# A graph layer and a mixture of experts in one kernel: spreading one group's layer-norm work over four expert tiles

## What is computed

```
x = x + gnn(layernorm(x), adj)                  # first half of the program
u = layernorm(x)
topk_vals, topk_idx = top_k(u @ gate_w + gate_b, 2)
topk_w = softmax(topk_vals)
h = relu(u @ w1[e] + b1[e]);  expert_out = h @ w2[e] + b2[e]
y = u + sum over the two chosen experts of topk_w * expert_out
x = x + layernorm(y) * gamma + beta             # the second layer norm is the group work of this study
```

## Time and profile before

| | us |
|---|---|
| median of 3 runs | 888.42 |
| lowest and highest run | 888.24, 890.37 |
| the profiled execution | 883.51 |
| span of its trace | 881.0 |

### The profile page before, as it was taken

One profiled execution on the slowest core, in us unless ns is written; L12 is line 12 of the kernel. 1 busy time (PEld: TensorE's weight loads), 2 busy tenths in 40 slices (PEclk: granted clock), 3 DMA queues, 4 the chain that ended last, 5 costly groups with the idle time before them and its releaser, 6 DMA issues. The chain is left out here.

```text
span 881.0 us, 20052 instructions
## 1 busy us (share of the span) xinstructions
PE 771.3 (88%) x4739; PEld 590.4 (67%) x4740; DVE 619.3 (70%) x2448; ACT 527.7 (60%) x1123; POOL 550.9 (63%) x572
## 2 busy tenths in 40 slices
PE   5999999999999999961899999988878888888844
PEld 4577777777777777751677777766656666666621
DVE  3688999999999998866455554567665666665648
ACT  2599999999999999871233333444443343343435
POOL 2005777777677777675777777777765565565630
PEclk9999999999999999995899999999998889898969
DMA  5323343333333332215777667888887778767636
GB/s 153 97 73 109 120 122 121 118 121 116 105 118 116 119 95 75 74 58 146 215 207 199 199 206 238 260 239 231 247 239 215 225 215 236 216 198 221 188 131 215
DMA packets 104175, 145.23 MB, mean 165 GB/s; under 512 B 17537, under 2 KB 56855, under 8 KB 104119
## 3 DMA queue, kind: packets, MB, share of 16 engines
q1 hardware_dynamic: 84582, 109.16, 44.0%
q0 software_dynamic: 17344, 34.13, 11.1%
q10 hardware_dynamic: 2192, 1.31, 0.5%
HBM read 99.67 MB, written 46.81 MB: 166 GB/s over the span
## 5 line engine op out<-in xcount | busy, mean ns | idle before, releaser
L471 POOL DMA_INDIRECT combined<-tout,tdest x286 | 285.7, 999 | 129.9 <-issue 74.0
L458 POOL DMA_INDIRECT dispatched<-rows,slot_i x256 | 259.5, 1014 | 165.5 <-issue 145.6
L795 ACT ACTIVATE hid<-bank,wts 128x256 f32<-128x256 f32 x286 | 119.6, 469 | 236.5 <-PE bank L651 235.8
L1119 DVE SCALAR_TENSOR_TENSOR tout<-bank,gate,tin 128x128 f32<-128x128 f32 x286 | 86.9, 345 | 157.9 <-PE bank L666 156.7
L666 PE MATMUL bank<-wts,hid 128*128 128x128 f32 x1144 | 175.5, 299 | 0.0
L666 PEld LDWEIGHTS bank<-wts,hid 128*128 128x128 f32 x1144 | 147.2, 201 | 17.8 <-issue 1.5
L651 PE MATMUL bank<-tut,wts 128*128 128x256 f32 x572 | 155.4, 396 | 0.0
L506 PEld LDWEIGHTS bank<-w_sb,work 128*128 128x128 f32 x1024 | 123.1, 194 | 17.9 <-issue 14.6
L506 PE MATMUL bank<-w_sb,work 128*128 128x128 f32 x1024 | 126.3, 277 | 2.1 <-ACT work L774 2.1
L500 PE MATMUL bank<-agg,w_sb 128*128 128x512 f32 x256 | 124.8, 610 | 0.0
L651 PEld LDWEIGHTS bank<-tut,wts 128*128 128x128 f32 x572 | 103.0, 201 | 8.7
(11 more groups left out here) (159 smaller groups left out, 1046.8 us busy)
## 6 DMA issues: line engine op xcount, KB each, us to landing
wts<-in_w_exp SPq DMA_DIRECT2D x143, 257.0 KB
tin<-dispatched SPq DMA_DIRECT2D x143, 132.0 KB
moe<-combined SPq DMA_DIRECT2D x32, 512.0 KB, 4.6
xs<-in_x SPq DMA_DIRECT2D x32, 256.0 KB, 3.2
adj_sb<-in_adj_t SPq DMA_DIRECT2D x32, 256.0 KB, 3.3
rms_b<-r_row SPq DMA_DIRECT2D x32, 256.0 KB, 3.2
out<-agg SPq DMA_DIRECT2D x32, 256.0 KB, 4.2
combined<-tout,tdest POOLq DMA_INDIRECT x286
```

The lines of the kernel that those rows point to most:

```text
L458: nc.gpsimd.indirect_dma_start(dispatched, bass.IndirectOffsetOnAxis(slot_i[:, k, n:n + 1], 0), rows[:, k, n // TOPK, n % TOPK, :], None). ...
L471: nc.gpsimd.indirect_dma_start(combined, bass.IndirectOffsetOnAxis(tdest[:, k, a:a + 1], 0), tout[:, k, a, :], None, bounds_check=TOK * TO ...
L795: last = nc.scalar.activation(hid[:, n % 2, c, :], hid_ps[n % 2][:, c * TILE:(c + 1) * TILE], ACT.Relu, bias=wts[:, k, F + FC * D + c:F + ...
L1119: last = nc.vector.scalar_tensor_tensor(out=tout[:, k, a, :], in0=exp_ps[n % 2][:, a * D:(a + 1) * D], scalar=gate[:, n % 2, a:a + 1], in1 ...
```

## The change

`post_step` gets an argument `quarters`. In `mixed` it is now called behind each of the four tiles, each time with one number from 0 to 3. VectorE has in quarter 0 the scale, the offset and the sum of the two halves, in quarter 1 the statistics, in quarter 2 the multiplication by gamma, in quarter 3 the last addition. ScalarE has two of its four activations in quarter 1, the other two and the square root in quarter 2. SP keeps its whole post step, in quarter 3. TensorE has nothing in these steps. The second part: `tut_ps` is now banks 0 and 1 in turn, so a transpose waits for the copy of two tiles back, not of the last one. `y_ps`, used in the tail, moves to banks 0 to 2.

```
-        tut_ps, hid_ps, exp_ps = bank[0], bank[2:4], bank[4:6]
-        y_ps = (bank[1], bank[6], bank[7])
+        tut_ps, hid_ps, exp_ps = bank[0:2], bank[2:4], bank[4:6]
+        y_ps = bank[0:RING]
...
                 for k in range(RING * GB):
                     tile_step(i, t + k, 2)
-                    if k % GB == GB - 1:
-                        post_step(i, g + k // GB)
+                    post_step(i, g + k // GB, (k % GB,))
...
# SP
-                if has(i, g):
+                if 3 in quarters and has(i, g):
...
# TensorE, tile_step
-                    if n >= 1:
-                        pe.wait_ge(t_ut, count(i, n, 1, RING2 * m))
+                    if n >= 2:
+                        pe.wait_ge(t_ut, count(i, n - 1, 1, RING2 * m))
                     for a in range(TH):
-                        last = nc.tensor.transpose(tut_ps[:, a * P:(a + 1) * P], tin[:, k, a, 0:D],
+                        last = nc.tensor.transpose(tut_ps[n % 2][:, a * P:(a + 1) * P], tin[:, k, a, 0:D],
                                                    ident[:])
...
# ScalarE, post_step
+                for half in range(2):
+                    if 1 + half in quarters and has(i, g):
...
+                        for j in (2 * half, 2 * half + 1):
+                            last = nc.scalar.activation(n3[:, k, j, :], y_of(i, g, k)[:, j, :], ACT.Identity,
+                                                        bias=nb[:, 0, k, j:j + 1], scale=rs[:, 0, k, j:j + 1])
+                        if half == 1:
+                            last.then_inc(p_n, 1)
...
-                if has(i, g):
+                if 2 in quarters and has(i, g):
                     k = g % RING
                     act.wait_ge(p_bn, count(i, g + 1))
...
# VectorE, post_step
                 g = t
-                if has(i, g):
+                if 0 in quarters and (i is not None or 0 <= g < MIXED):
+                    k = g % RING
+                    dve.wait_ge(moe_in[k], count(i, g // RING + 1, 16, 1))
+                    nc.vector.tensor_tensor(moe[:, k, :, 0, :], moe[:, k, :, 0, :], moe[:, k, :, 1, :],
+                                            ALU.add).then_inc(p_sum, 1)
+                if 1 in quarters and has(i, g):
```

More of the change, by code:

```diff
@@ L386, in _, with post_step @@
                 sp.wait_ge(scattered[k], 16 * GB * TOPK * len(range(k, NG, RING)))
-            def post_step(i, t):
+            def post_step(i, t, quarters=range(GB)):
                 g = t + 2
-                if has(i, g):
+                if 3 in quarters and has(i, g):
                     k = g % RING
@@ L798, in tile_step, with post_step @@
                     last.then_inc(t_relu, 1)
-            def post_step(i, t):
+            def post_step(i, t, quarters=range(GB)):
                 g = t - 1
-                if has(i, g):
[L803 to L811, removed]
+                for half in range(2):
+                    if 1 + half in quarters and has(i, g):
+                        k = g % RING
+                        if half == 0:
+                            if g >= RING:
+                                act.wait_ge(p_g, count(i, g - RING + 1))
+                            act.wait_ge(p_nb, count(i, g + 1))
+                            act.nop(nofuse=True)
+                        for j in (2 * half, 2 * half + 1):
[3 more added lines that the diff above has]
+                            last.then_inc(p_n, 1)
                 g = t
-                if has(i, g):
+                if 2 in quarters and has(i, g):
                     k = g % RING
@@ L816, in post_step @@
                     nc.scalar.activation(sd[:, 0, k, :], bn[:, 0, k, :, 2], ACT.Sqrt, bias=ln_eps[:, 0:1],
[L817 to L818 removed]
+                                         scale=1.0 / D).then_inc(p_sd, 1)
             tiles_and_groups(act, tile_step, post_step, -1)
@@ L1100, in tile_step @@
                         dve.wait_ge(t_h, count(i, n - 1, 1, RING2 * m))
-                    nc.vector.tensor_copy(tut[:, n % 2, :], tut_ps[:, 0:TILE]).then_inc(t_ut, 1)
+                    nc.vector.tensor_copy(tut[:, n % 2, :], tut_ps[n % 2][:, 0:TILE]).then_inc(t_ut, 1)
                 n = t - 1
@@ L1122, in tile_step, with post_step @@
                     last.then_inc(t_out, 1)
-            def post_step(i, t):
+            def post_step(i, t, quarters=range(GB)):
                 g = t - 1
-                if has(i, g):
+                if 0 in quarters and has(i, g):
                     k = g % RING
@@ L1129, in post_step @@
                     nc.vector.reciprocal(rs[:, 0, k], sd[:, 0, k, :]).then_inc(p_rs, 1)
-                g = t - 1
-                if has(i, g):
-                    k = g % RING
                     dve.wait_ge(p_rs, count(i, g + 1))
@@ L1137, in post_step @@
                 g = t
-                if has(i, g):
+                if 0 in quarters and (i is not None or 0 <= g < MIXED):
+                    k = g % RING
+                    dve.wait_ge(moe_in[k], count(i, g // RING + 1, 16, 1))
+                    nc.vector.tensor_tensor(moe[:, k, :, 0, :], moe[:, k, :, 0, :], moe[:, k, :, 1, :],
+                                            ALU.add).then_inc(p_sum, 1)
+                if 1 in quarters and has(i, g):
                     k = g % RING
                     if summed_by_dve(i, g):
-                        dve.wait_ge(moe_in[k], count(i, g // RING + 1, 16, 1))
-                        nc.vector.tensor_tensor(moe[:, k, :, 0, :], moe[:, k, :, 0, :], moe[:, k, :, 1, :],
-                                                ALU.add).then_inc(p_sum, 1)
                         dve.wait_ge(p_sum, count(i, g + 1))
@@ L1157, in post_step @@
                         .then_inc(p_g, 1)
-                g = t - 2
-                if has(i, g):
+                if 3 in quarters and has(i, g):
                     k = g % RING
```

## The result

| | before | after |
|---|---|---|
| median | 889.19 us (4 runs, 888.24 to 890.37) | 849.62 us (4 runs, 847.04 to 855.23) |
| profiled execution, span | 883.51, 881.0 | 847.04, 845.3 |

The changed kernel takes 0.956 of the time of the one before (95% interval 0.951 to 0.962), some 40 us less. The forecast was 851 us and a span of 844.

A forecast was written before the change was run, and what follows sets the result against it. VectorE's post-step lump stalls TensorE; beneath lie two floors, POOL's scatters and SP's loads. Their chains put the last scatter at 808.2 and 809.3, so 37 us off 888.4 gives 851 us; range for 8 in 10, 842 to 872.

The forecast's parts named there:

- The lump on VectorE and TensorE's wait for the copy: Mixed stretch: quarters of at most 1.1 us replace VectorE's 3.36 us lump; TensorE's 39.2 us wait should be nearly gone.
- the second edit's step: Two transpose banks: alone they only move the 2.01 us wait to the first product (L651); no term of its own.
- SP's wait for ScalarE: SP's load of moe waits for ScalarE's normalising; these 33.0 us should go nearly whole, below 5 us left.
- The load of `moe`, five tiles ahead instead of eight: The sum moves three tiles earlier, leaving the load at least 12.9 us against 4.6 us needed; costed at nothing.
- The two rivals without a gain: TensorE held at each quarter, 888 us, chance 0.05; VectorE waits for moe in quarter 0, slower, chance 0.05.
- POOL as one floor: Expert stretch: 285 scatter steps of 1.29 us plus contention put the last scatter's start at 808.2.
- 8.8 us of contention: POOL scatters starting inside VectorE additions of two SBUF operands: 0.4 us for each of 22 post steps.
- SP as the other floor: SP's load chain: without 33.0 us of waits and 3.6 us before the transpose, last scatter at 809.3.
- The tail moves as a whole: What follows the last scatter has unchanged code and moves 37 us earlier; span 844.
- What would make it wrong: Mean clock below 0.9, tiles waiting for tin over some 10 us in total, or VectorE waiting for moe.
- the other signs: POOL's tout waits below 20 us, 37 or 38 scatters per 50 us, last near 809, more long scatters, clock near 1.00.
- The third limit: Rival: DMA capped at 0.85 (866 us) or clock dropping once per group (873 us); together chance 0.25, 860 to 880.

The follow-up runs named there:

- half the scatters: Changed kernel with the second of each tile's two scatters left out and moe loaded from input x; 845.12 us, ratio 0.956 to the kernel before.
- paired reads: SP reads two tiles' table entries at once: changed kernel 853.98 us, ratio 0.968; also with half the scatters left out, moe from x, 842.45 us, ratio 0.954.
- ScalarE's transfers with operands in PSUM: Changed kernel with ScalarE issuing the post step's moe load and out store, and gamma, beta and their product in PSUM; 1125.44 us, ratio 0.982 to the kernel before.

## Why the prediction held, point by point

*The lump on VectorE and TensorE's wait for the copy* (3.36 us, 39.2 us in all): right. The quarters alone take the wait away; the banks alone only move it to L651, as the second edit's step said, and win what the transposes' head start is worth. Their bound was 0.4 us for each of 22 post steps, 9 us, and 10.5 us were measured, with an interval of 5 to 14.

*SP's wait for ScalarE*, 33.0 us: gone whole. SP's last load of rows was to be issued at 794.9 and was at 794.21.

*The load of `moe`, five tiles ahead instead of eight*, costed at nothing: right, no wait for `moe` shows. *The two rivals without a gain*, a copy late by a quarter and a VectorE that waits for `moe`, did not come.

*POOL as one floor*: right. It was to be busy from the first scatter to the last, and was. The step of 1.29 us plus 8.8 us of contention gave 376.5 us; it took 378.5. The excess over 0.98 us per scatter sums to 292.5 - 286 x 0.98 = 12.2 us. In 560 to 808 us, 34 scatters began inside one of the three instructions of a post step with two SBUF inputs, with over 0.1 us of it left, and took 1.21 us in the mean, which makes 34 x 0.23 = 7.8 us; the others took 0.997 us, which makes 2.5 us more. That rest has the same cause, in an instruction that the argument had left out, the addition of beta to `xs`, 128x128 and with two SBUF inputs too:

```profile
710.27 1.20 POOL L470 DMA_INDIRECT combined<-tout,tdest  x1 [0.31 <-issue]
710.30 0.28 DVE L1111 TENSOR_TENSOR xs<-xs,beta_sb 128x128 f32 x1
```

All scatters of the expert stretch that took over 1.00 us began inside one of these four instructions or at most 0.03 us ahead of the addition of beta. The term of 8.8 us against a measured 10.8 (378.5 - 367.7) was near by its own cause; I had drawn it from one post step, so that it came so near is in part luck.

*SP as the other floor*: near, but not so near as the sum had it. Its chain was to end at 809.3, POOL's at 808.2. The load came as forecast; from there to the transposes it took 4.5 us (794.21 to 798.67) instead of 2.6. And the sum moved the last scatter as a whole with the transposes, though in the kernel before that scatter was POOL's own lateness: the last `tout` was ready at 840.71, 5.2 us ahead of 845.88.

```profile
840.10 0.61 DVE L1119 SCALAR_TENSOR_TENSOR tout<-bank,gate,tin 128x128 f32<-128x128 f32 x2 [0.55 <-PE bank L666]
```

With POOL in step the last scatter follows its `tout` by one step of 1.3 us, so this chain by itself should have been put near 805.4. Measured, the last `tout` is ready at 805.33 and would allow a last scatter at 806.6, against POOL's 810.91. So POOL was the later chain, by about 4 us, and not SP by 1.1; that SP's sum of 809.3 lies near the measured 810.91 is luck. POOL's own sum, 808.2, missed by 2.7 us, 0.7 at its first scatter (432.43 for 431.72) and 2.0 of contention. That the chains lie within a few us is why half the scatters, in a run of their own, gave only 3 us.

*The tail moves as a whole*: right within a microsecond; from the last scatter's start to the end of the span it is 35.1 us before (881.0 - 845.88) and 34.4 after (845.3 - 810.91). The profiled execution came 36.5 us earlier, the median 39.6; its executions range over 8 us, so that the forecast median is met within 1.4 us says no more than that it is met within this spread.

*What would make it wrong* named tiles that wait for `tin` more than 10 us in total. They wait 21.2 us, and the time is right all the same. That sign was badly chosen: VectorE and POOL have up to six tiles of buffers between them, and as long as POOL has scatters in hand, TensorE's waits cost nothing. The argument had SP as a floor within 1 us of POOL, and should itself have expected these waits. Of the other signs, POOL's waits for `tout` (10.7 us, below 20), the scatters in 50 us and the last scatter (810.91, forecast near 809) came as told; scatters over 1.1 us are 34 where they were 12; the clock is near 1.00 only in a part of the windows.

*The third limit* (DMA capped near 0.85, or the clock): DMA reached 0.86 to 0.89 and did not hold the kernel, since POOL never ran dry. The clock fell to 0.93 and 0.95 in the two windows from 650 to 750 us. There the slow tiles stand behind waits for rows of 2.76, 2.17 and 1.64 us, so such waits have taken the place of a part of the old ones.

Open: how much the second bank adds to the quarters (nothing to some 12 us), why SP needs 3.7 us in the mean behind a post step with paired reads, of which their longer read explains about 0.9, and whether ScalarE's transfers with operands in PSUM beat the change on a chip of the first kind. There it was not measured; on the other kind the ratio is 0.982 against 0.987, each on its own chip, with intervals that overlap.

## What to carry to other kernels

When a lump of hidden work stalls the pipeline around it, compare the lump with the slack of one step, not its total with the total idle time; cut into pieces shorter than a step's slack, the same work cost almost nothing here. Before expecting the whole of a removed stall, walk each queue alone from its first to its last instruction, the issuing queues too: here the scatters set the new time, and the chain of the loads ended some 4 us before them, so that lifting one floor gave little. Follow each chain with its own last steps, not with the lateness of another engine. A wait that shows up in the trace costs only if the floor's own queue runs dry.

## What the runs showed of the hardware that was not expected

An indirect transfer issued by GpSimd is held only at its start. If it starts while VectorE runs an instruction with two SBUF inputs, it takes about 0.98 us plus what is left of that instruction less 0.12 us (1.47 with 0.62 left, 1.37 with 0.51 left). Started shortly ahead, it can go either way: one that began 0.02 us ahead of a 128x512 instruction took 0.98 us, and VectorE's 0.70, but in the changed kernel five of the eight that began up to 0.03 us ahead of such an instruction, here always the addition of beta, took 1.15 to 1.20 us. None that began 0.05 us ahead or more took over 1.00. Instructions that take one of their two tensors from PSUM did not hold it: 59 scatters of the changed kernel began inside one that makes `tout`, and they took 0.983 us in the mean, the longest 0.99. The Trainium skill (SBUF — State Buffer, Who interferes with whom) says that a VectorE instruction with two SBUF inputs contends with a GpSimd instruction that reads SBUF, by an exclusive lock; it does not name an indirect transfer there. The traces agree for the start and show no lock for the rest of the transfer.

Chips differ by far more than kernels: in three comparisons the kernel before took 883 to 889 us, on two other chips 1147 and 1160 us, and on the latter the change was worth 1.3%, not 4.4%. The traces there show waits whose source is named "remote", in the untouched first stretch too. What slows those chips was not found; in the expert stretch it all but goes away with half the scatters (512.5 us from the first to the last with all of them, 379.0 and 361.7 with half).
